# One-load stacked products for the router and the second expert bias, and one more score bias carried as key rows

## The reference, cut to what matters

```python
x = x + softmax(LN(x) @ ctx.T) @ ctx                     # block 1
# block 2, hs = LN(x): 16 heads, 4 values each
Q, K, V = hs@q_w+q_b, hs@k_w+k_b, hs@v_w+v_b
attn = softmax(Q[..., :4] @ K.T / 2)
mla_out = concat(attn @ V, 0) @ o_w + o_b
probs = softmax(mla_out @ router_w + router_b)
topw, topi = top_k(probs, 2)
combine = one_hot(topi) * topw / topw.sum()              # (b, s, 8)
h2[e] = gelu(mla_out @ w1[e] + b1[e]) @ w2[e] + b2[e]
x = x + hs + 0.3 * sum_e combine[..., e] * h2[e]
# block 3: similarity attention with ctx, features of 4*D @ W_qv
# block 4: one expert (E-1) of a second mixture, scaled by its softmax probability
```

## Time and profile before

| | |
|---|---|
| runs of the kernel | 160.58 us median of 3 (159.92, 160.58, 161.89) |
| the profiled execution | 158.49 us, of which its span is 156.7 us |
| PE busy | 145.9 us (93%) in 1255 products, loads 115.9 us |
| DVE, ACT, POOL busy | 109.9, 99.9, 50.5 us |
| granted TensorE clock | 0.999 over the span |
| chain that ended last | PE 68%, DVE 14%, ACT 9%, issue 4%, POOL 3% |
| DMA | 8.00 MB, mean 51 GB/s |

### The profile page before, as it was taken

The page is one execution under the profiler, slowest core; times in us unless marked ns, Lnnn a source line. Parts: engine busy times, 40 slices in busy tenths (PEclk is TensorE's granted clock), DMA queues, the critical chain, the costliest instruction groups (busy, mean ns, idle before and its releaser), DMA issues.

```text
span 156.7 us, 3840 instructions
## 1 busy us (share of the span) xinstructions
PE 145.9 (93%) x1255; PEld 115.9 (74%) x1255; DVE 109.9 (70%) x411; ACT 99.9 (64%) x218; POOL 50.5 (32%) x155
## 2 busy tenths in 40 slices
PE   7999995897999899999999999999999899998893
PEld 5676872564766647567998999799899789687682
DVE  4858899969887649844429666556867996755763
ACT  8886675385498687999389264866630046855380
POOL 7498900433245474499600000500011201300100
PEclk9999999999999999999999999999999999999999
DMA  3538700743557523000100000000000000000022
GB/s 112 148 58 275 223 2 0 151 122 72 111 133 180 131 50 56 19 6 0 36 0 4 0 0 0 0 4 0 2 4 0 2 0 0 4 0 0 2 67 67
DMA packets 11070, 8.00 MB, mean 51 GB/s; under 512 B 1867, under 2 KB 10155, under 8 KB 11051
## 3 DMA queue, kind: packets, MB, share of 16 engines
q1 hardware_dynamic: 11051, 7.76, 20.0%
HBM read 5.26 MB, written 1.70 MB: 44 GB/s over the span
## 4 chain that ended last, share of the span: by engine, by line
PE 68%; DVE 14%; ACT 9%; issue 4%; POOL 3%; POOLq 0%; ACTq 0%
PE ps L1105 63%; DVE nmax L888 4%; DVE qbd L882 2%; ACT qbd L604 2%; PE ps L1396 1%; PE ps L1423 1%; ACT L766 1%; ACT L588 1%; DVE stats L790 1%; POOL xn L552 1%; PE ps L1145 1%; DVE res L857 1%; POOL xn L550 1%; POOL xn L546 1%; ACT pr L636 1%
## 5 line engine op out<-in xcount | busy, mean ns | idle before, releaser
L1001 DVE SCALAR_TENSOR_TENSOR vpad<-ps,comb,vpad 128x128 f32<-128x128 f32 x64 | 18.3, 343 | 11.7 <-PE ps L1105 11.7
L888 DVE TENSOR_REDUCE nmax<-ps 128x4 f32<-128x512 f32 x32 | 20.7, 684 | 5.2 <-PE ps L1105 5.0
L576 POOL TENSOR_TENSOR rstd<-veps,power 128x2 f32<-128x2 f32 (+1 forms) x6 | 4.8, 806 | 49.2 <-DVE veps L800 49.2
L667 ACT ACTIVATE pexp<-ps 128x512 f32<-128x512 f32 x32 | 18.1, 593 | 3.5 <-PE ps L1105 3.4
L1105 PE MATMUL ps<-w2s,qbd 128*128 128x128 f32 x128 | 16.2, 278 | 0.5 <-DVE vpad L1001 0.5
L1105 PEld LDWEIGHTS ps<-w2s,qbd 128*128 128x128 f32 x128 | 15.3, 192 | 1.3 <-issue 1.1
L1105 PEld LDWEIGHTS ps<-w2s,vpad 128*128 128x128 f32 x128 | 14.9, 192 | 0.5 <-ACT vpad L717 0.2
L1105 PE MATMUL ps<-w2s,vpad 128*128 128x128 f32 x128 | 15.1, 276 | 0.0
L717 ACT ACTIVATE qbd<-ps,b1o 128x512 f32<-128x512 f32 x16 | 9.9, 694 | 6.5 <-PE ps L1105 6.5
L1105 PE MATMUL ps<-kst,qbd 128*128 128x128 bf16 x128 | 11.2, 219 | 2.6 <-DVE nmax L888 2.6
L1105 PE MATMUL ps<-ao,w_lo 128*128 128x512 f32 x32 | 13.6, 424 | 0.0
(11 more groups left out here) (236 smaller groups left out, 344.6 us busy)
## 6 DMA issues: line engine op xcount, KB each, us to landing
...
```

The lines of the kernel that those rows point to most:

```text
L576: pool.tensor_tensor(out=rstd[:, i, seqs(u)], in0=veps[:, i, seqs(u)], in1=power[:, seqs(u)], op=ALU.pow).then_inc(s[f"ln{i}_rstd"], 1)
L667: act.activation(pexp[:, n % 3, :], ps[:, 2 + n % 2, :], ACT.Exp, scale=KPH ** -0.5).then_inc(s["p_ok"], 1)
L888: dve.tensor_reduce(nmax[:, b, g, :], ps[:, n % 2, :].rearrange("p (j t) -> p j t", t=S), axis=AX.X, op=ALU.max, negate=True).then_inc(s[" ...
L1001: dve.scalar_tensor_tensor(out=x2[:, a + i, :], in0=ps[:, 2 + k % 2, i * D:(i + 1) * D], scalar=comb[:, a + i, e:e + 1], in1=x2[:, a + i, ...
```

## The change: what it does

Four edits and a new order. First, `STACKED` goes from 2 to 1: the selector product is left only for group 0, and `mrow` on POOL copies three blocks of rows instead of two. Second, the router takes the stacked tile `ao2` in place of `aoT`, with weights of 16 columns (a rounded high part and the rest), one load for each sequence instead of two; the halves are added on DVE. It now waits for `ao2_ok` instead of `aod_in`. Third, the expert bias becomes one product a half: `comb3` holds the weights three times (high, low, high), one transpose makes 96 rows, and `b2s` is a 96 x 512 matrix with the bias of each expert in its sequence's columns. Twelve small loads (`b2l`) replace one. Fourth, tiles for this are cleared and filled: a POOL memset, two more ACT copies in `oT`, four more DVE instructions in `combine` over both halves, two in `router:0`, and one in each `router`. The plan is a new one throughout; the warm-up products in it go from 45 to 38, and one product `hot:2,2` is added.

```diff
-STACKED = 2
+STACKED = 1
...
-        rwo = sb("rwo", [P, E0])
+        rwo = sb("rwo", [P, 2, E0], FP32R)
+        woT2 = sb("woT2", [D, LANES, 2, GROUPS * KPH])
...
-        combT = sb("combT", [E0, NHALF, T])
+        NB = HALF * E0
+        comb3 = sb("comb3", [P, NHALF, 3, NB], FP32R)
+        combT = sb("combT", [3 * NB, NHALF, S], FP32R)
+        b2raw = sc[0][0:3 * NB, :, :].rearrange("p b c -> p (b c)")[:, 0:HALF * D]
...
-        b2s = sb("b2s", [E0, D])
+        b2s = sb("b2s", [3 * NB, HALF * D], FP32R)
...
+            z_msp warm:1 z_den b2l warm:1 z_const warm:2 a_v:0 warm:2 spare warm:4 a_v:1 p1_parts:1 a_k z_v:0 warm:4 p1_stats:0
...
+            warm:1 p1_ln:0 warm:1 a_q:0 warm:1 z_sel:1 warm:1 p1_norm1:0 z_v:2 z_q:0 z_q:1 p1_av:1 setup p1_parts:2 p1_T2:0 a_q:1
+            warm:2 p1_ctx:2 warm:2 p1_qk:0 p1_ln:1 oT warm:3 p1_split:0 a_q:2 z_identb p1_v:0 p1_scores:2 p1_norm1:1 warm:1 rows:0
+            rows:1 p1_T2:1 rows:2 rows:3 p1_qk:1 p1_split:1 s1:0,0 dw:0 msp:0 fold:0 mrow:0 p1_soft:2 s1:0,1 fold:1 p1_pT:2 s1:0,2
+            s1:0,3 p1_av:2 fold:2 p1_v:1 mT:0 p1_ln:2 s1:1,0 fold:3 s2:0,0 p1_norm1:2 s1:1,1 s2:0,1 s1:1,2 s2:0,2 p1_T2:2 s1:1,3
+            av:0,0 av:0,1 p1_qk:2 mT:1 s2:0,3 p1_split:2 s2:1,0 s1:2,0 s1:2,1 p1_v:2 av:0,2 s2:1,1 s1:2,2 a_q:3 av:0,3 s2:1,2 un:0
...
+            s1:7,0 s2:4,2 s2:4,3 mT:5 s2:5,0 s1:7,1 av:4,1 ctxw:1 mT:6 av:4,2 ao2:0 av:4,3 s1:7,2 s1:7,3 un:4 s2:5,1 s2:5,2 den:4
+            norm:4 av:5,0 s2:5,3 s2:6,0 un:5 router:0 av:5,1 combine:0 av:5,2 av:5,3 s2:6,1 norm:5 p4_ctx:0 s2:6,2 den:5 p4_ctx:1
+            mrow:6 mT:7 av:6,0 av:6,1 s2:6,3 m1:0,0,0 s2:7,0 w1:1 av:6,2 av:6,3 msp:7 un:6 s2:7,1 s2:7,2 av:7,0 mrow:7 s2:7,3
+            av:7,1 fb av:7,2 norm:6 norm:7 w1:2 w1:3 av:7,3 un:7 den:6 w1:4 cT:0 den:7 x2_init:0 m1:0,0,1 m1:0,1,0 m1:0,1,1
+            gelu:0,0 gelu:0,1 ao2:1 acc:0,0 b2:0 w1:5 acc:0,1 gelu:0,2 w1:6 gelu:0,3 m1:0,2,0 m1:0,2,1 m2:0,0 m2:0,1 router:1
...
-            sp.dma_start(b2s[:, :], b2).then_inc(s["w2_in"], 16)
...
+            def load_b2():
+                sp.wait_ge(s["power_ok"], 2)
+                for r in range(0, 3 * NB, E0):
+                    b = r // E0 % HALF
+                    sp.dma_start(b2raw[r:r + E0, b * D:(b + 1) * D], b2).then_inc(s["w2_in"], 16)
...
+                pool.memset(b2raw[:, :], 0.0)
...
+                for a in range(2):
+                    act.activation(woT2[:, :, a, :].rearrange("p j (g v) -> p j g v", v=KPH),
+                                   ps[:, 0, 0:LAT].rearrange("p (g j v) -> p j g v", g=GROUPS, v=KPH), ACT.Copy)
...
-                act.activation(combT[:, h, :], ps[0:E0, (7, 4)[h], :], ACT.Copy).then_inc(s["cT_ok"], 1)
+                act.activation(combT[:, h, :], ps[0:3 * NB, (7, 4)[h], 0:S], ACT.Copy).then_inc(s["cT_ok"], 1)
...
-                dve.tensor_scalar(rwo[:, :], ps[:, 4, 0:E0], upper[:, 0:1], None, ALU.mult)
+                a = did(dve.tensor_copy(rwo[:, 0, :], ps[:, 4, 0:E0]))
+                after(a)
+                dve.tensor_tensor(out=rwo[:, 1, :], in0=ps[:, 4, 0:E0], in1=rwo[:, 0, :].bitcast(FP32), op=ALU.subtract)
...
+                    a = did(dve.tensor_tensor(out=pb[:, hs, :], in0=v[:, :, 0:E0], in1=bias[:, :].unsqueeze(1).to_broadcast([P, HALF, E0]), op=ALU.add))
+                    after(a)
+                    a = did(dve.tensor_tensor(out=pb[:, hs, :], in0=v[:, :, E0:2 * E0], in1=pb[:, hs, :], op=ALU.add))
...
+                if h == 0:
+                    dve.wait_ge(s["w2_in"], 16 * (1 + 3 * HALF))
+                    a = did(dve.tensor_copy(b2s[:, :], b2raw[:, :]))
+                    after(a)
+                    r = slice(2 * NB, 3 * NB)
+                    dve.tensor_tensor(out=b2s[r, :], in0=b2raw[r, :], in1=b2s[r, :].bitcast(FP32), op=ALU.subtract)
...
+                dve.wait_ge(s["comb_ok"], 2 * h + 1)
+                vals = comb[:, hs, :].rearrange("p b e -> p (b e)")
+                a = did(dve.tensor_copy(comb3[:, h, 0:3:2, :], vals.unsqueeze(1).to_broadcast([P, 2, NB])))
+                after(a)
+                dve.tensor_tensor(out=comb3[:, h, 1, :], in0=vals, in1=comb3[:, h, 0, :].bitcast(FP32), op=ALU.subtract).then_inc(s["comb_ok"], 1)
...
-                pe.wait_ge(s["aod_in"], 16 * LANES * (h + 1))
+                pe.wait_ge(s["ao2_ok"], h + 1)
+                pe.wait_ge(s["rwo_ok"], 1)
...
-                    last = mm(ps[:, 4, n * E0:(n + 1) * E0], aoT[:, h, n * S:(n + 1) * S], rwo[:, :])
+                    last = mm(ps[:, 4, n * 2 * E0:(n + 1) * 2 * E0], ao2[:, h, n * S:(n + 1) * S], rwo[:, :, :].rearrange("p a e -> p (a e)"))
...
-                for n in range(HALF):
-                    last = nc.tensor.transpose(ps[0:E0, (7, 4)[h], n * S:(n + 1) * S], comb[:, h * HALF + n, :], ident[:, :])
+                nc.tensor.transpose(ps[0:3 * NB, (7, 4)[h], 0:S], comb3[:, h, :, :].rearrange("p r c -> p (r c)").bitcast(FP32),
+                                    ident[:, :]).then_inc(s["cT_ps"], 1)
...
-                for n in range(HALF):
-                    last = mm(ps[:, 5, n * D:(n + 1) * D], combT[:, h, n * S:(n + 1) * S], b2s[:, :])
-                last.then_inc(s["b2_ps"], 1)
+                mm(ps[:, 5, :], combT[:, h, :], b2s[:, :]).then_inc(s["b2_ps"], 1)
```

More of the change, by code:

```diff
@@ L304, in build @@
         plan = stages_of("""
[L305 to L324, removed]
@@ L333, in build @@
[L333 to L335 removed]
+            z_msp warm:1 z_den b2l warm:1 z_const warm:2 a_v:0 warm:2 spare warm:4 a_v:1 p1_parts:1 a_k z_v:0 warm:4 p1_stats:0
+            warm:3 p1_ctx:0 z_v:1 p1_stats:1 warm:1 z_sel:0 warm:2 p1_T:0 warm:2 p1_norm:0 warm:1 p1_stats:2 warm:1 p1_norm:1
@@ new lines, in build @@
+            s1:0,3 p1_av:2 fold:2 p1_v:1 mT:0 p1_ln:2 s1:1,0 fold:3 s2:0,0 p1_norm1:2 s1:1,1 s2:0,1 s1:1,2 s2:0,2 p1_T2:2 s1:1,3
+            av:0,0 av:0,1 p1_qk:2 mT:1 s2:0,3 p1_split:2 s2:1,0 s1:2,0 s1:2,1 p1_v:2 av:0,2 s2:1,1 s1:2,2 a_q:3 av:0,3 s2:1,2 un:0
+            s1:2,3 av:1,0 av:1,1 s1:3,0 s2:1,3 msp:1 s1:3,1 hot:2,2 s1:3,2 mT:2 fr av:1,2 s2:2,0 s1:3,3 s1:4,0 s2:2,1 un:1 s2:2,2
+            mrow:1 den:0 av:1,3 av:2,0 s1:4,1 mT:3 norm:0 s2:2,3 msp:2 s1:4,2 av:2,1 s1:4,3 s2:3,0 mrow:2 den:1 av:2,2 s2:3,1
@@ new lines, in build @@
+            ctxw:0 s1:5,0 s2:3,2 msp:3 s1:5,1 un:2 av:2,3 av:3,0 norm:1 av:3,1 mrow:3 msp:4 s2:3,3 mrow:4 s1:5,2 mT:4 den:2 s1:5,3
+            av:3,2 s1:6,0 un:3 av:3,3 msp:5 s1:6,1 s2:4,0 s1:6,2 den:3 da:0 s2:4,1 norm:2 norm:3 s1:6,3 msp:6 av:4,0 w1:0 mrow:5
+            s1:7,0 s2:4,2 s2:4,3 mT:5 s2:5,0 s1:7,1 av:4,1 ctxw:1 mT:6 av:4,2 ao2:0 av:4,3 s1:7,2 s1:7,3 un:4 s2:5,1 s2:5,2 den:4
+            norm:4 av:5,0 s2:5,3 s2:6,0 un:5 router:0 av:5,1 combine:0 av:5,2 av:5,3 s2:6,1 norm:5 p4_ctx:0 s2:6,2 den:5 p4_ctx:1
@@ L433, in store @@
                 sp.dma_start(out.rearrange("b t d -> t b d")[:, seqs(u), :], y[:, seqs(u), :]).then_inc(s["stored"], 16)
-            run({"p1_parts": parts, "dw": double_w, "da": double_a, "p5_end": store})
+            run({"b2l": load_b2, "p1_parts": parts, "dw": double_w, "da": double_a, "p5_end": store})
             sp.wait_ge(s["stored"], 16 * len(UNITS))
@@ L929, in logits @@
                 n = hs.stop - hs.start
-                v = ps[:, bank, 0:n * E0].rearrange("p (b e) -> p b e", e=E0)
+                w = E0 if bias is None else 2 * E0
+                v = ps[:, bank, 0:n * w].rearrange("p (b e) -> p b e", e=w)
                 dve.wait_ge(psum_ready, h + 1)
@@ L934, in logits @@
                 else:
-                    a = did(dve.tensor_tensor(out=pb[:, hs, :], in0=v, in1=bias[:, :].unsqueeze(1).to_broadcast([P, HALF, E0]), op=ALU.add))
+                    a = did(dve.tensor_tensor(out=pb[:, hs, :], in0=v[:, :, 0:E0], in1=bias[:, :].unsqueeze(1).to_broadcast([P, HALF, E0]), op=ALU.add))
+                    after(a)
+                    a = did(dve.tensor_tensor(out=pb[:, hs, :], in0=v[:, :, E0:2 * E0], in1=pb[:, hs, :], op=ALU.add))
                 after(a)
```

30 lines of the change are left out of this document (18 added, 12 removed).

## The result

The changed kernel took 161.44 us (median of 7 runs, 160.92 to 161.85), the kernel before 159.75 us beside it (7 runs, 159.20 to 161.89). The ratio is 1.0108, 95% interval 1.0077 to 1.0139: **slower by about 1.7 us**. The forecast was 1.4 us faster, so the two differ by 3.1 us. The forecast time, 159.2 us, was worked from a median of 160.58 for the kernel before; beside the changed kernel that median is 159.75, and the number alone makes the miss look smaller. The profiled execution of after took 161.44 us, with a span of 159.7. That of before was 1.3 us under its median, so the two traces lie 3.0 us apart where the medians lie 1.7 apart.

The account below looks back on a forecast made before the run. PE was taken to bound the kernel from 60 to 120 us. Of its savings 3.4 us lay behind `den:4`; less 1.35 for its delay and 0.6 at the gelus, 1.4 us gained: median 159.2 us, range 156.8 to 161.4.

Parts of the forecast that it names:

- What bounds the kernel: From 60 to 120 us PE is busy without a gap; a product removed there is worth its start-to-start pitch.
- What the change takes from PE: Selector products, router, transposes and bias, less 0.1 us for `hot`: 4.8 us taken from PE.
- The third rival: Stacked 16-column float32r products cost as much as 512-column ones; 1.1 us less gained, 160.3 us; chance 8%.
- The front: Early stages: ACT's order costs 0.4 us and row copies on PE 0.4, so the third `p1_split` is 0.8 us late.
- The rule on the port: DVE and POOL block each other on the shared SBUF port; up to 0.4 us per collision, left out of the sum.
- The wait for the doubled rows: ACT stands at `ao2:0` for SP's doubled rows until 59.9 us, so `den:4` starts 1.35 us late.
- The moved order as a whole: Behind `den:4`, two `av` moved behind it and two `s1` ahead, costed at 0.2 us net against the gain.
- rival 2: Row copies on POOL bound each sequence before `s2:b,1`; kernel 0.7 us slower, 161.3 us; chance 17%.
- The first activation: At the experts' first gelus, PE waits before `m2:0,0` for both gelus; 0.6 us given back.
- Costed at nothing: DVE's added work around `router:0`, covered by 2.8 us; `ao2:1` gating `router:1` just fits; tail swaps fall into idle time.
- The tail: From 123 us PE's order is the same; swaps on ACT, POOL and DVE fall into idle time, cost nothing.
- DVE's additions: Conversion and subtraction of `b2s`, at most 0.67 us each, plus 0.7 small instructions; 2.8 us before the transposes covers 2.0.

Follow-up runs that it names:

- experiment 6: Changed kernel with STACKED = 2 (two row copies) and the old kernel's order, keeping the stacked bias product and one-load router: 159.29 us, ratio 0.9992 to the kernel before.
- experiment 9: Kernel before, its own code, in the changed kernel's order without the b2l loads: 162.94 us, ratio 1.0228 to the kernel before.
- experiment 7: Changed kernel in its new order with one line changed, STACKED = 2 (two row copies): 161.53 us, ratio 1.0123 to the kernel before.
- experiment 5: Kernel before in its own order with one line changed, STACKED = 1 (third row copy, eight selector products fewer): 164.03 us, ratio 1.0276.
- experiment 1: Changed kernel, but POOL waits for DVE's four small oT instructions before clearing z_q:1: 160.43 us, ratio 1.0037 to the kernel before.
- 8: Changed kernel in its new order with STACKED = 2, and POOL waiting for DVE's oT before z_q:1: 160.56 us, ratio 1.0042 to the kernel before.
- Experiment 2: Changed kernel with one POOL swap, the row copies of sequence 5 ahead of weight split w1:0: 161.29 us, ratio 1.0083 to the kernel before.
- experiment 10: As experiment 6, but DVE's two b2s roundings moved from router:0 to behind s1:6,3: 158.20 us, ratio 0.9935 to the kernel before.
- 4: Changed kernel with all its edits in the order of the kernel before, only needed stages moved: 163.32 us, ratio 1.0202 to the kernel before.
- 12: As experiment 10, but the two b2s roundings put earlier, behind ctxw:1: 158.44 us, ratio 0.9911 to the kernel before.

## Why the prediction was wrong

**What bounds the kernel: right for before, and the trap.** PE is dense from 60 to 120 us in the kernel before. "A product taken out of this stretch is worth its pitch as long as nothing else comes due" holds only as far as its condition does: in the sixth experiment 2.5 us came off PE and 2.5 us of waits came in.

**What the change takes from PE: right in sum.** 4.2 us of busy time by the page against 4.8. By the pages of experiments 9 and 7 the stacked products give 3.3 of it (145.9 to 142.6; 3.2 forecast) and the eight selector products 0.9 (142.6 to 141.7; 0.7 in the old order, experiment 5; 1.7 forecast). Why these give half, no run shows. Router 0.45 in the second half (0.4 forecast), one bias product and one transpose for four, at the records' usual lengths. The third rival (products not cheaper) is refuted.

**The front: the first step that failed.** The step "0.8 us later; bounds 0 and 1.2" for the third split measured 2.4 us, outside both bounds; without the collision it is 1.3 (experiment 1), still 0.1 over the upper bound. It was costed by ACT's order and PE's order alone. The clearing on POOL was costed at nothing, "under one of its early fills"; but POOL had no idle time there, so 0.52 us of clearing moved the fills of `z_q:1`, which the new order had put next to `oT`, further into DVE's way. The collision was worth 1.0 us of the kernel (experiments 1 and 8). By the starts of the first split, 0.3 us of it come with the order and 0.5 with the clearing (experiments 1, 9 and 7). The rule on the port was weighed in the prediction, but at POOL's row copies, and only for DVE instructions with two SBUF inputs. Here the held instructions have one tensor input in SBUF, and the fills beside them read none. With two inputs it did come, but in `combine`, beside POOL's weight splits (experiment 6), where the prediction did not look. The Trainium skill ("SBUF — State Buffer", section "SBUF: two separate sides") names DVE operations "in a 2-port perf mode" beside those with two inputs; whether these three are of that kind, no run here shows. It says that the holder keeps the ports "for the whole instruction"; here the measured 1.84 us is over twice the longest single fill (0.74 us), so the measurement decides: in three traces (after, experiments 7 and 9) DVE went on only when the whole run of fills had ended.

**The wait for the doubled rows: right in sign, mis-sized.** `den:4` was forecast 1.35 us late and was 3.4. Of the 2.0 us between, the first experiment gives back 1.2. The forecast named ACT's wait for the doubled rows as the cause; ACT shows none at `ao_hi` there (it stood behind `mT` until 62.04, and by the forecast's own sum the doubled rows landed at 58.22 + 2.42 - 0.59 + 1.9 = 61.95, 0.1 us before). Experiment 2 shows that wait, 0.19 us, once the rows of sequence 5 are early. So several paths (doubling, rows behind `w1:0`, `mT`) end within 0.5 us of each other there, and which comes last in after stays open.

**The moved order as a whole: not costed.** The sum gave the new order 0.2 us for two `av` and two `s1`. It loses 3.5 us by itself (experiment 9), of which the collision is some 0.3. PE's waits for `mT` are 1.7 us of it, in front of `s2:1,0` and `s2:5,0`, which the plan moved close behind `mT:1` and `mT:5`; `pT` is 0.8, and the rest lies in smaller waits. This is the largest missing term, and the step that failed most: 3.5 us against 1.0 in the forecast (0.8 at the third split and 0.2). Against it stand 1.7 us from the stacked products (experiments 9 and 7) and 0.2 from the selector products with the third copy (experiment 7 and the changed kernel). Reading it needed each pair of producer and consumer in the new plan against the old one, with PE's work between them: rival 2's own table of 1.7 to 3 us did this, for the copies alone.

**The first activation: right mechanism, mis-placed and short.** 0.6 us at `m2:0,0` was forecast; 1.18 us came two stages earlier, at `m1:0,2,0`, because PE waited there for the first gelu. The sixth experiment has it in the old order, at 0.7.

**Costed at nothing.** The twelve loads: right. The tail: right, the delay grew by 0.2. `ao2:1` gating `router:1`: right, PE has no wait there. DVE's additions: wrong. The cover of 2.8 us was read in the old order from `comb` to the transposes, and 2.0 us of new work were set against it; in the sixth experiment the stacked weights came 3.5 us late, since collisions with POOL came on top. The forecast itself said who is late if the cover goes. Moving the roundings alone gave 0.9 us back (experiment 10).

**Rival 2** (row copies bound each sequence) had 17%, at 161.3. The time came out within 0.2 us of it, but by another road: that is luck. As a mechanism it is true in the old order, 4.4 us (experiment 5), and in the new order the third copy costs no more than the selector products give back (7 against the changed kernel, 8 against 1). That is what the new order buys, at a price of 3.5 us.

**The account**, in ratios to the kernel before: the new order 1.0228 (9); the products bring it to 1.0123 (7); the third copy for the selectors to 1.0108 (the changed kernel). In the old order: all edits 1.0202 (4), third copy 1.0276 (5), products 0.9992 (6), products without their rounding in the middle 0.9935 and 0.9911 (10, 12). The cheapest set is the old order, two copies, the stacked products, and the rounding elsewhere: 1.0 to 1.4 us faster than before. Open: which path sets `den:4` in the new order, and what each wait is worth of the 3 us that the order costs beside the collision.
